# Edge stage of a graph network: twelve transposes in one run ahead of the edge-feature products

## The reference, cut to what matters

```python
ei = concatenate([x[src], edge_attr], axis=-1)          # (E, 320)
core = maximum(ei @ W1 + b1, 0.0) @ W2 + b2
gate = sigmoid(ei @ Wg + bg)
agg = segment_sum(gate * core, dst, num_segments=N)      # first layer
x = layernorm(x + layernorm(agg + x) * gamma + beta)     # (written out in the reference)
# second layer: two hops over the normalised graph, then a linear layer and a log_softmax
x = layernorm(x + log_softmax(hop(hop(x)) @ W.T + b))
```

## Time and profile before

| | us |
|---|---|
| median of three runs | 2490.89 |
| span of the profiled execution | 2488.3 |
| TensorE busy (93% of the span) | 2315.5 |
| VectorE busy (77%) | 1927.1 |
| ScalarE busy (66%) | 1651.3 |
| GpSimd busy (66%) | 1641.2 |

### The profile page before, as it was taken

The page is one execution under the profiler, slowest core; times in us unless marked ns, Lnnn a source line. Parts: engine busy times, 40 slices in busy tenths (PEclk is TensorE's granted clock), DMA queues, the critical chain, the costliest instruction groups (busy, mean ns, idle before and its releaser), DMA issues. The chain is left out here.

```text
span 2488.3 us, 48732 instructions
## 1 busy us (share of the span) xinstructions
PE 2315.5 (93%) x16053; PEld 1833.1 (74%) x16053; DVE 1927.1 (77%) x4467; ACT 1651.3 (66%) x3119; POOL 1641.2 (66%) x1581
## 2 busy tenths in 40 slices
PE   7889999999999999999999996689999999999973
PEld 3369999999999999999999995145555554555542
DVE  6748878888887877888888989998888874447673
ACT  1158888888888889889998996454577751013232
POOL 0177777777777777777777773355676763777773
PEclk9989999999999999999999998799999999999996
DMA  6465656655556556656666662345556635776652
GB/s 220 163 211 169 170 168 173 172 171 169 168 170 169 170 168 188 179 171 186 183 186 183 183 186 84 99 123 135 149 153 162 181 88 178 263 238 211 211 163 79
DMA packets 276158, 422.41 MB, mean 170 GB/s; under 512 B 127618, under 2 KB 198548, under 8 KB 273860
## 3 DMA queue, kind: packets, MB, share of 16 engines
q0 software_dynamic: 90368, 281.11, 39.3%
q1 hardware_dynamic: 170028, 116.99, 15.4%
q10 hardware_dynamic: 15512, 21.17, 2.5%
HBM read 354.78 MB, written 64.37 MB: 168 GB/s over the span
## 5 line engine op out<-in xcount | busy, mean ns | idle before, releaser
L801 POOL DMA_INDIRECT gathered<-p_table,src_t x784 | 773.4, 987 | 275.6 <-issue 196.8
L801 POOL DMA_INDIRECT gathered<-hop_table,src_t x576 | 584.0, 1014 | 336.0 <-issue 154.5
L976 PE MATMUL banks<-w_hi,hidden_hi 128*128 128x256 f32 x1568 | 458.3, 292 | 3.9 <-ACT banks L1313 3.8
L976 PE MATMUL banks<-w_lo,hidden_hi 128*128 128x256 f32 x1568 | 441.8, 282 | 0.0
L976 PE MATMUL banks<-w_hi,hidden_lo 128*128 128x256 f32 x1568 | 441.2, 281 | 0.0
L1426 ACT CAST counts<-banks 128x686 f32 (+3 forms) x382 | 295.8, 774 | 155.6 <-PE banks L1038 76.4
L1796 DVE TENSOR_TENSOR room<-banks,gate 128x512 f32<-128x512 f32 x392 | 265.3, 686 | 76.5 <-PE banks L976 75.8
L822 POOL TENSOR_TENSOR msg_lo<-room,msg_hi 128x512 fp32r<-128x512 f32 x196 | 250.7, 1279 | 93.4 <-ACT msg_hi L1306 92.3
L1299 ACT ACTIVATE hidden_hi<-banks 128x512 fp32r<-128x512 f32 x392 | 235.0, 600 | 114.2 <-PE banks L953 111.5
L976 PEld LDWEIGHTS banks<-w_hi,hidden_hi 128*128 128x128 f32 x1568 | 297.3, 190 | 5.9 <-issue 4.2
L976 PEld LDWEIGHTS banks<-w_lo,hidden_hi 128*128 128x128 f32 x1568 | 298.3, 190 | 0.0
(11 more groups left out here) (224 smaller groups left out, 5304.3 us busy)
## 6 DMA issues: line engine op xcount, KB each, us to landing
ea<-in_edge_attr SPq DMA_DIRECT2D x196, 128.0 KB
counts_saved<-counts SPq DMA_DIRECT2D x16, 1568.0 KB, 9.7
ring<-counts_saved SPq DMA_DIRECT2D x16, 1568.0 KB, 7.6
gathered<-p_table,src_t POOLq DMA_INDIRECT x784
p_table<-p_t ACTq DMA_DIRECT2D x48, 256.0 KB, 2.6
hop_table<-parts SPq DMA_DIRECT2D x12, 896.0 KB
gathered<-hop_table,src_t POOLq DMA_INDIRECT x576, 2.9
x_saved<-x_room SPq DMA_DIRECT2D x7, 896.0 KB, 6.1
```

The lines of the kernel that those rows point to most:

```text
L801: pool.indirect_dma_start(out=rows[:, n % slots, j, :], out_offset=None, in_=table[:, :], in_offset=bass.IndirectOffsetOnAxis(ap=src_t[:, ...
L976: last = nc.tensor.matmul(banks[:, 4 + half, j % 2 * H:(j % 2 + 1) * H], lhs, rhs, start=False, stop=n == len(products) - 1, skip_group_ch ...
```

## The change

`hidden_product` is split. A new function `turn_rows` does the eight transposes of the gathered rows, all of bank 0 and then all of bank 1; the first one of each bank opens it. `hidden_product` then accumulates its two products for each bank onto them, and the last product of each bank raises the semaphore. `turn_ea` moves from the end of the step to right behind `core_product`, so that its four transposes and the eight of `turn_rows` stand in one run. The other engines' streams are the same as before.

```diff
-            def hidden_product(turn, s, g):
-
-                pe.wait_ge(S["ea_ready"], g + 1)
+            def turn_rows(turn, s, g):
+
                 pe.wait_ge(S[f"p_gathered{s}"], 16 * TILES * (turn + 1))
                 for k in range(KC):
                     columns = slice(k * P, (k + 1) * P)
                     wait_count(pe, S["hidden_ready"], 2 * g + k - 1)
-                    nc.tensor.matmul(banks[:, k, :], w_e_hi[:, columns], ea_turned_sb[:, s, :], start=True, stop=False)
-                    nc.tensor.matmul(banks[:, k, :], w_e_lo[:, columns], ea_turned_sb[:, s, :], start=False, stop=False)
                     for j in range(TILES):
-                        last = nc.tensor.matmul(banks[:, k, j * P:(j + 1) * P], gathered[:, s, j, columns], ident[:, :],
-                                                start=False, stop=j == TILES - 1, is_transpose=True)
+                        nc.tensor.matmul(banks[:, k, j * P:(j + 1) * P], gathered[:, s, j, columns], ident[:, :],
+                                         start=j == 0, stop=False, is_transpose=True, skip_group_check=True)
+
+            def hidden_product(turn, s, g):
+
+                pe.wait_ge(S["ea_ready"], g + 1)
+                for k in range(KC):
+                    columns = slice(k * P, (k + 1) * P)
+                    nc.tensor.matmul(banks[:, k, :], w_e_hi[:, columns], ea_turned_sb[:, s, :], start=False, stop=False,
+                                     skip_group_check=True)
+                    last = nc.tensor.matmul(banks[:, k, :], w_e_lo[:, columns], ea_turned_sb[:, s, :], start=False, stop=True,
+                                            skip_group_check=True)
                     last.then_inc(S["hidden_product"], 1)
...
                 def step(i, s):
                     at_group(core_product, i, s, 0)
+                    at_group(turn_ea, i, s, 4)
+                    at_group(turn_rows, i, s, 2)
                     at_group(hidden_product, i, s, 2)
                     at_group(gate_product, i, s, 2)
                     at_group(scatter_stage, i, s, -1)
-                    at_group(turn_ea, i, s, 4)
```

## The result

The changed kernel takes 2535.37 us (five runs, 2533.36 to 2538.35) against 2490.82 us for the kernel before: ratio 1.018, 95% interval 1.0169 to 1.0191, 44.6 us slower. The forecast was 2527 us, range 2508 to 2538. The profiled execution has a span of 2533.6 us, 45.3 us above that of before.

A forecast was written before the change was run, and what follows sets the result against it. The prediction took TensorE, fully busy at 7.00 us a step, to bound the edge stage. Grouping 0, ring 34 and late steps 2 gave +36 us on 2490.9: 2527 us, range 2508 to 2538.

The forecast's parts named there:

- TensorE's own work: TensorE's instructions in an edge-stage step: none added or removed, so it remains 7.00 us.
- the grouping: Three runs of four transposes become one of twelve on TensorE: 0 us taken for it.
- The recorded 0.48 us behind a run: Product after a run of transposes, recorded 0.48 us against 0.39: said to take over the last transpose's time, no real price.
- The delay of the hidden bank: ScalarE's relu of bank 0 starts 2.03 us behind the core products instead of 1.16, 0.87 us later.
- The ring's price from waited steps: Steps where TensorE already waited for the seed gave 2.23 and 2.92 us; step 7.18 us, +0.18 over 190 steps: 34 us.
- Late steps: A dozen steps with node work, where ScalarE or VectorE is late, may cost more: 0 to +5 us, taken +2.
- the ring: Core products, transposes, hidden bank 0, relu, bias seed, next core products: a closed loop setting the step at 7.18 us.
- The copy of bank 7: ScalarE's copy emptying the bank for the moved `turn_ea`: 1.0 us of cover left, cost nothing.
- The other moves: `turn_ea` and `turn_rows` earlier on TensorE, GpSimd's gathers 0.43 us later: all taken to cost nothing.
- The second-ring rival: Later gathers on GpSimd or VectorE's late message close another loop: 0.15 us in 190 steps, 2555 us, chance 8%.
- The clock: Rival: TensorE's clock falls to 1.2 GHz in the run of transposes, 257 us more, 2748 us, chance 1%.
- What was to show it: Trace signs: relu at 2.03 us, TensorE waiting 0.1 to 0.2 us for the seed in nearly every step, step 7.18 us.

The follow-up runs named there:

- e2: The changed kernel with ScalarE's bias seed for the next core products moved ahead of the relu of bank 0: 2505.04 us, ratio 1.0062.
- e11: e10 with two of each hidden bank's four transposes put between its two products, five runs of transposes a step instead of three: 2509.23 us.
- e1: The changed kernel with `turn_ea` back at the end of the step, so two runs of transposes (8 and 4): 2493.43 us, ratio 1.0017.
- e3: The kernel before with the eight scatter products moved ahead of `hidden_product`, no transpose moved: 2544.74 us, ratio 1.0224.
- e9: The changed kernel with ScalarE's bias seed moved right behind the relu of bank 0: 2510.91 us, ratio 1.008.
- e10: The kernel before with ScalarE's bias seed moved right behind the relu of bank 0: 2505.08 us, ratio 1.0054.
- e4: The kernel before with ScalarE's bias seed moved ahead of the relu of bank 0: 2503.20 us, ratio 1.0051.
- e6: The kernel before with the seed right behind the relu of bank 0, where the kernel before takes 2640.0 us: 2622.16 us, ratio 0.992.

## Why the prediction was right

**TensorE's own work: right.** No gain from the grouping was forecast; e2 shows 0.003 us a step lost, e11 at most 0.013 us a change. The recorded 0.48 us behind a run was indeed the last transpose's time under another name.

**The delay of the hidden bank: right.** Relu at 2.03 us against 2.03. e1 and e3 moved it to 1.60 and 2.10 us, and the step followed to 7.01 and 7.28 us.

**The ring's price from waited steps: right in its mechanism, small in its size.** Relu to core product 2.24 us against 2.23. The core products behind a wait took 2.93 and 2.95 us by turns instead of the 2.92 read from a single step, and the mean undisturbed step is 7.21 us, not 7.18. That term of the sum, 34 us, should have been 40 to 41 (195 distances x 0.21).

**Late steps: right by its sum, in part by luck.** The forecast was +2 us; the stage grew by 43.7 us, 41 of which are the ring, so 2.7 are left. By start distances, the steps that run more than 0.06 us over their kernel's base sum to 5.4 us where they summed to 3.1. It went both ways, as the text said. Steps 123, 147, 165 and 183, behind the node instruction of 1.71 us on ScalarE, ran 2.9 us over their base together instead of 0.9; three others (126, 43 and 107) grew by 0.7 us in all; steps 186, 193 and 194 shrank by 0.5.

**The copy of bank 7: wrong.** The prediction left 1.0 us of cover ahead of the moved `turn_ea` and took nothing for it. That holds in undisturbed steps. In the four steps just named the node instruction uses it up, and there TensorE waits 0.48 us each for this copy, 1.9 us in all (the last wait shown under the result), and not for the seed. In the changed kernel it adds little to the time, for e1 and e3, with `turn_ea` at the end of the step, run 2.6 and 2.4 us over in the same four steps. With the ring open it shows: 4.7 us in e9 over e10, and 1.6 in e2 over e4, where other steps give most of it back.

**The other moves and rivals: right, with a reservation.** The gathers and the landing cost nothing visible. The second-ring rival named VectorE's message; it did not close in the changed kernel, but the late steps of e2, e4, e9 and e10 bear its marks. The clock did not fall: the changed kernel has 1.00 in both stretches, with a run of twelve transposes in every step. The row of the set-up that the prediction leaned on was weaker evidence than it said, since its sixteen transposes are of 62 x 62 elements:

```profile
38.40 1.21 PE L882 MATMUL banks<-ident,x_room 62*128 62x62 f32 x16
```

**What was to show it.** The wait for the seed in nearly every step is there in the start distances, but not in the wait list, as I had put it: the list shows it three times. The remaining 1.6 us (45.3 less 43.7) lie before and behind the edge stage and have no cause that I can name.

**Left open.** On e6's chip VectorE's message waited 54.0 us in 55 times for something that the profile calls remote. What that is was not tried. It can't be the whole of the chip's longer time: e6's span is 119.5 us above that of e10, the same kernel, and 96.7 us of this lie behind the edge stage.

## What to carry to other kernels

When an engine is fully busy, an order that adds no work can still cost time: look for what waits for the result that now comes later, follow that engine's queue in order until it comes back to the busy engine, and sum the ring. Steps in which the busy engine already waited once, for any reason, give the ring's latency ready measured. Before opening a ring by moving an instruction forward, ask what it pushes back: here a seed moved between two relus opened a ring worth 41 us (e9 against the changed kernel) and gave 16 us of it back in late steps. And when an instruction moves forward, measure its cover in the steps with the longest foreign work ahead of it, not in the usual one: 1.0 us was enough in most steps and too little in four.

## What the runs showed of the hardware

**A short wait vanishes from the busy share.** The changed kernel reads 100.00 us of 100 busy while TensorE waits 0.13 us in each step: its products are recorded 0.28 us long and start 0.12 us apart.

**VectorE and GpSimd hold each other up.** Line 1809/1817, the same instruction on the same shapes, and line 822, in the kernel before (first two rows) and after (last two); ns are min/median/max.

```profile
L1809 DVE TENSOR_TENSOR hot_window<-iota,lo_t x196: 674/1277/2370, 167.5 to 1533.3; 128x512 fp32r<-128x512 f32 x196
L822 POOL TENSOR_TENSOR msg_lo<-room,msg_hi x196: 1183/1195/1652, 167.7 to 1532.7; 128x512 fp32r<-128x512 f32 x196
```

```profile
L1817 DVE TENSOR_TENSOR hot_window<-iota,lo_t x196: 670/678/1189, 168.0 to 1577.3; 128x512 fp32r<-128x512 f32 x196
L822 POOL TENSOR_TENSOR msg_lo<-room,msg_hi x196: 1192/1512/1549, 168.2 to 1576.8; 128x512 fp32r<-128x512 f32 x196
```

In the steps shown above and in the earlier trace rows, GpSimd began at 803.64 and VectorE at 803.83 before; after, VectorE begins at 521.56 and GpSimd at 521.77. VectorE's median falls from 1.28 to 0.68 us, and GpSimd's grows from 1.20 to 1.51. The one that starts second pays, and this holds within one kernel too. In the kernel before, GpSimd is first in 114 groups, with medians of 1.29 us for VectorE and 1.19 for GpSimd; VectorE is first in 68, with 0.68 and 1.47.

The Trainium skill says so on the page "SBUF — State Buffer", section "Who interferes with whom": a VectorE instruction with two inputs in SBUF contends with a GpSimd instruction that reads SBUF, and whoever issues first gets the shared port pair for the whole instruction while the other blocks. Lines 1809/1817 and 822 are such a pair, and the rows agree: in both orders the second one grows by most of the time that the two overlap (by 0.62 us of 0.75 for VectorE before, by 0.32 of 0.46 for GpSimd after, in medians). Neither is on the ring that sets the undisturbed steps; what it costs in late ones was not tried.
